# Cross attention: one context tile of both heads per exp and clip, the clip on GpSimd, the sum on VectorE, the second score pass on 64 rows

## The reference

```
k = apply_rope(k, cos, sin)
attn = einsum('bhnd,bhsd->bhns', q, k) * scale
attn = jnp.clip(attn, -11.0, 11.0)
attn = softmax(attn, axis=-1)
out = einsum('bhns,bhsd->bhnd', attn, v)
out = out.transpose(0, 2, 1, 3).reshape(b, n, INNER) @ Wo + bo
```

## Time and profile before

| | |
|---|---|
| median of 3 runs | 3293.78 us (3291.59 to 3296.01) |
| the profiled execution | 3288.86 us, span 3287.0 us |
| cross attention's loop in it | about 714 to 2655 us |
| busy in the span | PE 2925.8, DVE 2456.0, POOL 1690.2, ACT 1440.9 us |
| mean granted TensorE clock | 0.964 |

### The profile page before, as it was taken

How to read it: one execution, slowest core, us unless ns; L and a number is a source line. 1 busy time by engine, 2 the same in 40 slices (tenths; PEclk the granted TensorE clock), 3 DMA queues, 4 the chain that set the end, 5 groups by cost and what they waited for, 6 DMA issues and landing times. The chain is left out here.

```text
span 3287.0 us, 52895 instructions
## 1 busy us (share of the span) xinstructions
PE 2925.8 (89%) x17208; PEld 2104.2 (64%) x17256; DVE 2456.0 (75%) x3858; ACT 1440.9 (44%) x2076; POOL 1690.2 (51%) x1188
## 2 busy tenths in 40 slices
PE   5999999979888898998988988988988978999993
PEld 4888888755465564564564564564564548999993
DVE  3555555578888888888888888788878775588886
ACT  2222222254543543543553553553543533355553
POOL 1222222245655655656656656656646534466666
PEclk9999999989999999999999999999999989999996
DMA  9000000020110110110110110110110022266665
GB/s 250 14 15 14 15 14 15 20 65 14 26 46 14 26 46 14 26 47 14 26 47 14 26 47 14 26 47 14 26 40 20 20 84 102 88 207 227 224 218 197
DMA packets 137039, 197.69 MB, mean 60 GB/s; under 512 B 16992, under 2 KB 96864, under 8 KB 136736
## 3 DMA queue, kind: packets, MB, share of 16 engines
q1 hardware_dynamic: 115696, 160.52, 16.3%
q10 hardware_dynamic: 14224, 14.58, 1.8%
q0 software_dynamic: 6816, 18.75, 1.6%
HBM read 118.54 MB, written 41.71 MB: 49 GB/s over the span
## 5 line engine op out<-in xcount | busy, mean ns | idle before, releaser
L1082 ACT ACTIVATE raw<-b_ps 128x1024 f32<-128x1024 f32 x512 | 505.0, 1022 | 461.5 <-PE b_ps L854 394.8
L1226 DVE TENSOR_SCALAR raw<-raw 128x1024 f32<-128x1024 f32 x512 | 581.8, 1142 | 115.1 <-ACT raw L1082 112.7
L965 PE MATMUL b_ps<-raw 128*64 128x512 f32 x2048 | 518.1, 628 | 112.9 <-DVE raw L1226 112.5
L853 PE MATMUL b_ps<-b_QQ,b_KT 128*128 128x512 f32 x1024 | 433.5, 423 | 15.7 <-DMA b_QQ<-b_QQ 8.7
L823 POOL TENSOR_TENSOR b_acc<-b_acc,raw 128x512 f32<-128x512 f32 x256 | 370.9, 1449 | 85.5 <-DVE raw L1226 53.5
L854 PE MATMUL b_ps<-b_QQ,b_KT 128*128 128x512 f32 x1024 | 404.1, 395 | 0.0
L827 POOL TENSOR_TENSOR b_acc<-b_acc,raw 128x512 f32<-128x512 f32 x256 | 389.7, 1522 | 20.1
L806 POOL TENSOR_TENSOR b_QQ<-raw,b_QQ 128x512 fp32r<-128x512 f32 x128 | 165.4, 1292 | 410.5 <-ACT b_QQ L1032 410.5
L965 PEld LDWEIGHTS b_ps<-raw 128*64 128x64 f32 x2048 | 127.8, 139 | 371.5 <-issue 203.9
L853 PEld LDWEIGHTS b_ps<-b_QQ,b_KT 128*128 128x128 f32 x1024 | 193.4, 189 | 251.2 <-issue 193.6
L1682 PE MATMUL c_ps<-c_xT_l,c_w_h 128*128 128x256 f32 x1504 | 305.9, 287 | 8.6 <-DVE c_xT_l L1952 4.2
(11 more groups left out here) (264 smaller groups left out, 7095.5 us busy)
## 6 DMA issues: line engine op xcount, KB each, us to landing
c_raw<-in_L_ffn_W_dram SPq DMA_DIRECT2D x117, 512.0 KB, 4.2
b_QQ<-b_QQ SPq DMA_DIRECT2D x128, 256.0 KB, 3.4
xs<-zeros ACTq DMA_DIRECT2D x1, 10140.0 KB, 70.6
c_xg<-xs SPq DMA_DIRECT2D x39, 260.0 KB, 6.0
b_rows<-in_ctx_dram SPq DMA_DIRECT2D x9, 1024.0 KB, 7.3
a_xt<-in_x_dram SPq DMA_DIRECT2D x72, 64.0 KB, 2.2
b_rows<-x SPq DMA_DIRECT2D x9, 512.0 KB, 6.8
x<-a_x1t SPq DMA_DIRECT2D x64, 64.0 KB, 1.9
```

The lines of the kernel that those rows point to most:

```text
L853: pe.matmul(bank(key, a), k, QQ[:, n % 2, hh, 0, :], start=True, stop=False)
L965: mm = pe.matmul(bank(key)[hh * HD:(hh + 1) * HD, :], V[:, t, (2 * p + hh) * HD:(2 * p + hh + 1) * HD], probs[:, at_step(j, hh), (t % 2) * ...
L1082: ins = act.activation(probs[:, at_step(j, hh), :], both(key), ACT.Exp, scale=SCALE)
L1226: dve.tensor_scalar(pr, pr, HI, LO, ALU.min, ALU.max).then_inc(clipped, 1)
```

## The change

A slot is now one context tile of both heads: A holds tile 2j, B tile 2j + 1, head 0 in the first bank and head 1 in the second. `scores` makes the first pass of both slots (L837 of the changed file), and then the second pass of both (L845), which takes only the 64 partitions with the high part of the keys: k low times q low is no longer computed. For that the odd heads have high and low swapped in `KT`, head 0 of a pair has its high part on partitions 0 to 63 and head 1 on 64 to 127, and only the high part of q is spread by DMA, right behind `q_hi`. POOL does all clips (L816), eight of 128x1024 a pair in place of its ten adds of 128x512. DVE does all adds (L1218, L1221), seven of 128x1024 a pair, in place of eight clips, two adds of step 3 and two joins. `acc` has two buffers and `accf` is gone. PV waits for each slot's clip by itself. Exp waits for PV and the add of two steps ago.

```diff
-        def at_step(j, hh):
-
-            return 2 * ((j + 1) % 2) + hh
+        def at_step(j, a):
+
+            return 2 * ((j + 1) % 2) + a
...
-        acc = sb("b_acc", [P, 2, B])
-        accf = sb("b_accf", [P, 2, B])
+        acc = sb("b_acc", [P, 2, 2, B])
...
-                    sp.wait_ge(q_ready, b * (2 * PG) + n + 1)
+                    sp.wait_ge(qh_ready, b * (2 * PG) + n + 1)
                     for hh in range(2):
                         here, there = slice(hh * HD, (hh + 1) * HD), slice((1 - hh) * HD, (2 - hh) * HD)
-                        sp.dma_start(QQ[there, n % 2, hh, :, :].bitcast(F32), QQ[here, n % 2, hh, :, :].bitcast(F32)
+                        sp.dma_start(QQ[there, n % 2, hh, 0, :].bitcast(F32), QQ[here, n % 2, hh, 0, :].bitcast(F32)
                                      ).then_inc(q_spread, 16)
...
-                            nat = knat[:, t % 2, :].rearrange("p (h a n) -> p h a n", a=2, n=HD)
-                            pool.tensor_tensor(nat[:, :, 1, :], krot[:, t % 2, :].rearrange("p (h n) -> p h n", n=HD),
-                                               nat[:, :, 0, :].bitcast(F32), ALU.subtract).then_inc(knat_ready, 1)
+                            nat = knat[:, t % 2, :].rearrange("p (q x n) -> p q x n", x=4, n=HD)
+                            pool.tensor_tensor(nat[:, :, 1:3, :],
+                                               krot[:, t % 2, :].rearrange("p (q a n) -> p q a n", a=2, n=HD),
+                                               nat[:, :, 0::3, :].bitcast(F32), ALU.subtract).then_inc(knat_ready, 1)
...
                         for p in range(PG):
-                            for j in range(3):
-                                for hh in range(2):
-
-                                    pool.wait_ge(clipped, b * (16 * PG) + (step(g, p, j) * 2 + hh + 1))
-                                    pr = probs[:, at_step(j, hh), :]
-                                    if j == 0:
-                                        pool.wait_ge(accf_ready, b * (4 * PG) + ((g * PG + p) * 2))
-                                        ins = pool.tensor_tensor(acc[:, hh, :], pr[:, 0:B], pr[:, B:2 * B], ALU.add)
-                                    else:
-                                        ins = pool.tensor_tensor(acc[:, hh, :], acc[:, hh, :], pr[:, 0:B], ALU.add)
-                                        links += 1
-                                        ins.then_inc(pchain, 1)
-                                        pool.wait_ge(pchain, b * (16 * PG // 2) + links)
-                                        ins = pool.tensor_tensor(acc[:, hh, :], acc[:, hh, :], pr[:, B:2 * B], ALU.add)
-                                    ins.then_inc(acc_ready, 1)
-                                    pool.wait_ge(acc_ready, b * (12 * PG) + ((g * PG + p) * 3 + j) * 2 + hh + 1)
+                            for j in range(4):
+                                for a in range(2):
+                                    pr = probs[:, at_step(j, a), :]
+                                    wait_drained(pool, ("s", g, p, j, a), b)
+                                    pool.sem_inc(consts, 1)
+                                    pool.tensor_scalar(pr, pr, HI, LO, ALU.min, ALU.max).then_inc(clipped, 1)
                                 if (g, p, j) == (1, 0, 0):
...
-                for hh in range(2):
-                    key = ("s", g, p, j, hh)
+                for a in range(2):
+                    key = ("s", g, p, j, a)
+                    t = 2 * j + a
                     wait_free(pe, key, b)
-                    if j == 0 and hh == 0:
+                    if j == 0 and a == 0:
                         pe.wait_ge(q_spread, b * (32 * 2 * PG) + 32 * (n + 1))
+                        pe.wait_ge(q_ready, b * (2 * PG) + n + 1)
                     if p == 0:
-
-                        for a in range(2):
-                            wait_drained(pe, ("kt", g, 2 * j + 1, a), b)
-                            wait_drained(pe, ("kt", g, 2 * j, a), b)
-                    for a in range(2):
-                        t = 2 * j + a
-                        k = KT[:, 2 * p + hh, t * P:(t + 1) * P]
-                        pe.matmul(bank(key, a), k, QQ[:, n % 2, hh, 0, :], start=True, stop=False)
-                        mm = pe.matmul(bank(key, a), k, QQ[:, n % 2, hh, 1, :], start=False, stop=True)
+                        for half in (1, 0):
+                            wait_drained(pe, ("kt", g, t, half), b)
+                    for hh in range(2):
+                        pe.matmul(bank(key, hh), KT[:, 2 * p + hh, t * P:(t + 1) * P], QQ[:, n % 2, hh, 0, :],
+                                  start=True, stop=False)
+
+                for a in range(2):
+                    key = ("s", g, p, j, a)
+                    t = 2 * j + a
+                    for hh in range(2):
+                        own = slice(hh * HD, (hh + 1) * HD)
+                        mm = pe.matmul(bank(key, hh), KT[own, 2 * p + hh, t * P:(t + 1) * P],
+                                       QQ[own, n % 2, hh, 1, :], start=False, stop=True)
                     fill(key, mm)
...
-                pe.wait_ge(accf_ready, b * (4 * PG) + (g * PG + p + 1) * 2)
+                pe.wait_ge(acc_ready, b * (16 * PG) + (step(g, p, 3) + 1) * 2)
                 for hh in range(2):
-                    mm = pe.matmul(bank(key)[hh * HD:(hh + 1) * HD, :], ones[:, :], accf[:, hh, :],
+                    mm = pe.matmul(bank(key)[hh * HD:(hh + 1) * HD, :], ones[:, :], acc[:, p % 2, hh, :],
...
-                                pe.wait_ge(clipped, b * (16 * PG) + (step(g, p, j) + 1) * 2)
-                                for t in (2 * j, 2 * j + 1):
+                                for a in range(2):
+                                    t = 2 * j + a
+                                    pe.wait_ge(clipped, b * (16 * PG) + step(g, p, j) * 2 + a + 1)
...
-                                                       probs[:, at_step(j, hh), (t % 2) * B:(t % 2 + 1) * B],
+                                                       probs[:, at_step(j, a), hh * B:(hh + 1) * B],
...
-                                        if before % 4 == 3:
-                                            act.wait_ge(accf_ready, b * (4 * PG) + (before // 4) * 2 + hh + 1)
-                                        else:
-                                            act.wait_ge(acc_ready, b * (12 * PG)
-                                                        + ((before // 4) * 3 + before % 4) * 2 + hh + 1)
-                                    ins = act.activation(probs[:, at_step(j, hh), :], both(key), ACT.Exp, scale=SCALE)
+                                        act.wait_ge(acc_ready, b * (16 * PG) + before * 2 + a + 1)
+                                    ins = act.activation(probs[:, at_step(j, a), :], both(key), ACT.Exp, scale=SCALE)
                                     drain(key, ins, 2)
...
-                                for hh in range(2):
-                                    n = step(g, p, j) * 2 + hh
-                                    at = (j, hh)
-                                    pr = probs[:, at_step(j, hh), :]
-                                    wait_drained(dve, ("s", g, p, j, hh), b)
-                                    dve.tensor_scalar(pr, pr, HI, LO, ALU.min, ALU.max).then_inc(clipped, 1)
+                                for a in range(2):
+                                    n = step(g, p, j) * 2 + a
+                                    at = (j, a)
+                                    pr = probs[:, at_step(j, a), :]
+                                    total = acc[:, p % 2].rearrange("p h n -> p (h n)")
+                                    if at != (0, 0):
+                                        dve.wait_ge(clipped, b * (16 * PG) + n + 1)
+                                    if at == (0, 1):
+                                        dve.tensor_tensor(total, probs[:, at_step(0, 0), :], pr, ALU.add).then_inc(acc_ready, 2)
+                                    elif j:
+                                        dve.wait_ge(acc_ready, b * (16 * PG) + n)
+                                        dve.tensor_tensor(total, total, pr, ALU.add).then_inc(acc_ready, 1)
                                     if 0 < p < PG - 1 and at == (3, 0):
                                         o_scaled(p - 1)
-                                    if j == 3:
-
-
-                                        for h2 in ((hh,) if p + 1 < PG else (0, 1)[:2 * hh]):
-                                            dve.wait_ge(clipped, b * (16 * PG) + n + 1)
-                                            e = probs[:, at_step(j, h2), :]
-                                            ins = dve.tensor_tensor(accf[:, h2, :], e[:, 0:B], e[:, B:2 * B], ALU.add)
-                                        if hh == 1:
-                                            link(ins, b)
-                                            for h2 in range(2):
```

(11 more changed lines are left out.)

18 lines of the change are left out of this document (7 added, 11 removed).

## The result

The changed kernel took 3219.6 us (median of 4 runs, 3218.3 to 3224.7), the kernel before 3293.3 in the same rounds: ratio 0.9777, 95% interval 0.9764 to 0.9791. That is faster by 2.2%, and outside the predicted range (3225 to 3400, point 3260). The profiled execution has a span of 3217.3 us against 3287.0, so 70 us went where 34 were forecast.

A forecast was written before the change was run, and what follows sets the result against it. No engine alone was the bound: PE waits for clips because DVE and POOL contend for an SBUF port. Per entry -8.6 - 20.9 + 24.0 + 1.2 = -4.3 us, times eight -34, gave 3260 us, range 3225 to 3400.

The forecast's parts named there:

- dear clip: Rival: the clip on POOL takes longer, slowing every pair; 3395 us at 1.7; chances 0.13 (1.35 to 1.7), 0.15 above.
- PE's own work: Score second passes on 64 rows in overlapping pairs save net 0.27 us a step, 8.6 us an entry.
- waits of before: PE's present waits for clips and at the sums, 167 us or 20.9 per entry, were to go.
- four boundaries, context split with them: New PE waits at pair boundaries, 4 x 2.7 us an entry, plus 3.2 in half 1 for ACT's context split.
- two half ends: End of each half: PE's stall of 2.92 us shrinks to about 1.4, so 2 x 1.4 an entry.
- clips of third and last steps: New PE waits for clips in the third and last steps, 5.2 us an entry.
- short gaps, first clips: Gaps under 0.3 us, 2 an entry; first clips behind POOL's bias add or power, 1.2.
- The spread "nothing": The shorter spread DMA of the queries starts earlier and is asked for later: no gain or loss.
- waiting for slot B's exp before A's second pass costs nothing: In scores, this wait is free as long as PE is behind ACT, having PV and first passes in between.
- No overlap of the 64-row pairs: Rival: paired 64-row score matmuls run one after the other, +0.47 us a step, about 3300 us; chance 0.06.
- No boundary wait: Rival: PE alone sets the pace at pair boundaries, saving 2.8 us a pair, 3115 us; chance 0.05.
- Half clock at the new boundaries: Rival: PE falls to half clock behind new boundary waits, 1.6 us each, +51 less 15, 3296 us; chance 0.13.

The follow-up runs named there:

- e7: Changed kernel with VectorE clipping the sum to itself four times behind each half's last add, putting the stall back; 3318.0 us, ratio 1.0082.
- e1: Changed kernel with the second score pass back on 128 rows and low parts of the queries spread too; 3260.6 us, ratio 0.9894.
- e9: Changed kernel with second pass on 128 rows, low parts spread too, and slot A's four score matmuls before slot B's; 3235.2 us, ratio 0.9820.
- e5: Kernel before with only the order of its eight score matmuls changed: first passes of both heads, then second passes; 3312.2 us, ratio 1.0053.
- e6: Changed kernel with tile A's second passes right behind its first passes, then tile B's; 3195.0 us, ratio 0.9694.
- e3: Changed kernel with ScalarE's o_hi moved behind the first two exponentials of pair p+2, VectorE's low part behind it; 3117.9 us, ratio 0.9461.
- e2: Kernel before with only the 64-row second passes in pairs, the key layout and the shorter spread; 3322.3 us, ratio 1.0088.
- e8: Changed kernel with the late o_hi, and keys_values of the next half moved ahead of a half's last PV; 3105.7 us, ratio 0.9419.
- e4: Changed kernel with clips on VectorE and 1024-wide adds on GpSimd, except a half's last add; 3385.1 us, ratio 1.0269.

## Why the prediction was wrong

The direction came out, and so did most of the mechanism (no dear clip, a new wait at the boundary, a shorter stall at the end of a half); the size was half. The direction was partly luck: with the measured -4.3 for PE's own work in place of -8.6, and all else as forecast, the sum would have been 0. Per batch entry (8 of them) the prediction had -8.6 for PE's own work and +4.3 for waits. From PE's records over the 16 halves of the loop I took each stretch without an instruction, by the step it stands in, and, of what is left, the part at low clock:

| us per entry | forecast | measured |
|---|---|---|
| PE's own work | -8.6 | -4.3 |
| waits of before | -20.9 | -22.9 |
| four boundaries, context split with them | 10.8 + 3.2 | 10.7 |
| two half ends | 2.8 | 0.4 |
| clips of third and last steps | 5.2 | 5.4 |
| short gaps, first clips | 2.0 + 1.2 | 2.4 |
| low clock | 0 | -0.6 |
| sum | -4.3 | -8.9 |

- **PE's own work: over-sized.** The step's scores fell from 2.04 to 1.81 us in the median, 0.23 where 0.27 was forecast (the 64-row pairs follow each other at 0.33 us and not at 0.23), and 0.18 in the mean; PV's matmuls grew by 1.5 us an entry. I take what the mean adds for short waits that the profile counts into durations; no run separates them. This error was +4.3 and hid part of the others.
- **The boundary wait: right in place and cause, mis-sized.** 1.97 and 1.98 us in half 0 (forecast 2.7 to 2.8), 3.99 and 2.72 in half 1, where ScalarE's context split and more work of VectorE come on top; the 3.99 is beyond the 3.5 that the prediction named as a sign of being wrong, but the four with the split are 10.7 us, not 14.0. I charged each of three adds 0.5 us for meeting a clip; their mean is 1.32 against 1.22 alone, 0.1 each. VectorE's add is hardly lengthened beside GpSimd's clip; the clip is (1.44 in the mean, 1.04 at its shortest). -3.3 us an entry.
- **The half end: the step that failed most in kind.** "A stall of about 1.4 (1.15 + 1.22, less what the last PV covers)" put the clip and the add in one row ahead of the sums. The last PV waits for the same clip and covers the add; the clip's wait had its own term already. -2.4 us an entry in waits: the sums wait 0.4 us an entry and not 2.8. e7 shows the price of such a stall to be double, by the clock.
- **The spread "nothing": wrong.** It is little against the kernel before only (8.7 us of waits there, none in the changed kernel); e1 and e9 show 55 and 68 us of waits for it once the other part is there. In the median it lands 3.4 us behind its issue in e1 and in the kernel before, with both parts of q, and 2.4 in the changed kernel. Likewise "waiting for slot B's exp before A's second pass costs nothing" and the silence on the later fill: e5 prices that delay at 16 us in the kernel before, and e6 at some 105 in the changed one (25 gained in spite of 80 us more work of PE; part of that work may have filled waits).
- **Waits of before** were 22.9, not 20.9: I left out those at the first passes (15.7 us over the kernel).
- **Rivals.** Dear clip: out, 1.04 us. No overlap of the 64-row pairs: out, 0.67 us for four. No boundary wait: out as it stood, but e3 makes that case at 3118, where it was forecast at 3115; so close it is by chance, since e3 still has 45.7 us of waits for the clip. Half clock at the new boundaries: it happened, e3 gives 41 us for it; but lost clock fell by as much where the waits of before had stood, mostly at the half ends, so the net is -5 and not +36.

What stays open: the 4 to 5 us by which the sums for e3 and e7 miss, how e2's loss divides, and what lies behind the mean of PE's own work.

## What to carry to other kernels

Before pricing a shorter matmul sequence, write down when each output that another engine waits for is complete; in a chained pipeline that moment can be worth more than the work saved, and the same edit can be a loss alone and a gain beside another. Price the whole path of an edit that fills a wait, too: e8 filled one and opened another behind it. Look at which small copies stand ahead of the next tile's first operation in an in-order queue: moving one `o_hi` behind two exponentials gave more than the whole change. And at an end, ask what each last operation waits for before adding durations: two that wait for the same one lie beside each other.

## What the runs showed of the hardware

- A stall of PE of 3.2 us was followed by stretches at 1.2 GHz that cost about as much again (e7: +47 us of waits, +53 of clock).
- GpSimd's clip of 128x1024 with two limits takes 1.04 us at its shortest, its two-input add of the same size 2.34 (e4), VectorE's clip 0.68 and its add 1.22 alone. The Trainium skill, GPSIMD Engine Reference (Performance versus the Vector engine), has a body of at most two operations per element at 1.03 cycles an element; with the 0.26 us of the earlier trace rows added that is 1.1 us for the clip, an estimate, and the trace agrees with it. The same page (Key points) calls VectorE about twice as fast for elementwise work; here that holds for the add (2.34 against 1.22) and not for the clip (1.04 against 0.68).
- Putting a 64-row pair between 128-row matmuls twice a step instead of once costs 0.36 us a step in the median (e6: 2.17 against 1.81 us).
- The two 64-row matmuls of 512 columns of a pair, on different halves of the array, start 3 ns apart; a pair takes 0.33 us where a 128-row matmul takes 0.23 (changed kernel, medians of the steps).
